# Reordering the queues of a fused attention and expert layer: fp32 products together, m behind f2, expert 0 last

## The reference

```python
q, k, v = xn @ q_w, xn @ k_w, xn @ v_w                      # 32 columns each
scores = (q @ k.T) * decay_weights                          # strictly causal, decays with distance
att = (scores @ v) @ o_w.T * out_scale
logits = xn @ router_w + router_b + load_balancer           # 4 experts, the best 2 by softmax
e0 = silu(xn @ sw_w1) * (xn @ sw_w3) @ sw_w2                # 512 hidden
e1 = gelu(sym @ me_c1w + me_c1b) @ me_c2w + me_c2b          # sym: three linear maps of xn; 256 hidden
h2 = layer_norm(syn + attn)                                 # syn, attn: linear maps of xn
h2 = layer_norm(h2 + relu(h2 @ ce_f1w + ce_f1b) @ ce_f2w + ce_f2b)
e2 = h2 @ ce_gen_w + ce_gen_b
e3 = gelu(xn @ ml_w1 + ml_b1) @ ml_w2 + ml_b2               # 512 hidden
out = x + att + sum of the two chosen experts, weighted
```

## Time and profile before

| what | us |
|---|---|
| median of 3 runs | 475.91 (475.39 to 476.07) |
| the profiled execution's own time | 475.9 |
| its span, first to last instruction | 474.1 |
| PE busy | 456.7 (96%) |
| DVE busy | 389.5 (82%) |
| ACT busy | 271.3 (57%) |
| POOL busy | 251.8 (53%) |

### The profile page before, as it was taken

The page is one execution under the profiler, slowest core; times in us unless marked ns, Lnnn a source line. Parts: engine busy times, 40 slices in busy tenths (PEclk is TensorE's granted clock), DMA queues, the critical chain, the costliest instruction groups (busy, mean ns, idle before and its releaser), DMA issues.

```text
span 474.1 us, 9536 instructions
## 1 busy us (share of the span) xinstructions
PE 456.7 (96%) x2892; PEld 381.9 (81%) x2892; DVE 389.5 (82%) x1292; ACT 271.3 (57%) x534; POOL 251.8 (53%) x370
## 2 busy tenths in 40 slices
PE   3879999999999999999999999999999999999994
PEld 2758888897888889788888878878898888878884
DVE  4567988979798897988889798888979888886994
ACT  3582846548284663829457383845728375482831
POOL 4692645737265572726657273664726357471541
PEclk9999999999999999999999999999999999999999
DMA  7300010010101001010000101001010100100000
GB/s 264 18 6 19 2 45 2 1 45 2 46 0 37 7 0 44 0 44 0 21 23 0 44 0 44 0 3 41 0 44 0 44 0 0 44 1 22 3 24 22
DMA packets 18786, 11.43 MB, mean 24 GB/s; under 512 B 1136, under 2 KB 18256, under 8 KB 18768
## 3 DMA queue, kind: packets, MB, share of 16 engines
q1 hardware_dynamic: 18480, 11.20, 8.8%
q10 hardware_dynamic: 288, 0.01, 0.0%
HBM read 6.80 MB, written 4.19 MB: 23 GB/s over the span
## 4 chain that ended last, share of the span: by engine, by line
issue 48%; POOL 36%; POOLq 11%; PE 2%; DVE 1%; ACT 1%; DMA 1%; DVEq 0%
POOL hid3l L430 14%; POOL hidl L434 9%; POOLq L398 7%; POOL n L400 5%; POOL xn L400 5%; POOLq L443 2%; POOLq L396 2%; POOL rstd_u L444 1%; DMA ROW<-rows 1%; POOL negmean_x L395 0%; POOL negmean_c L395 0%; DVE falling L604 0%; PE TR L892 0%; POOL WL L416 0%; ACT hid L523 0%
## 5 line engine op out<-in xcount | busy, mean ns | idle before, releaser
L967 PE MATMUL S<-xh,WH 128*128 128x512 f32 x224 | 98.7, 441 | 2.1 <-ACT hid L523 2.1
L969 PE MATMUL S<-xh,WL 128*128 128x512 f32 x224 | 88.5, 395 | 0.0
L968 PE MATMUL S<-xl,WH 128*128 128x512 f32 x224 | 88.1, 393 | 0.0
L430 POOL TENSOR_TENSOR hid3l<-hid,hid3h 128x512 fp32r<-128x512 f32 x64 | 80.2, 1283 | 0.0
L394 POOL TENSOR_TENSOR veps_x<-mv_x,eps 128x4 f32<-128x4 f32 x16 | 3.2, 199 | 120.9 <-DVE mv_x L582 120.9
L560 ACT ACTIVATE hid<-S,me_b 128x512 f32<-128x512 f32 x32 | 22.1, 689 | 67.4 <-PE S L969 67.3
L925 PE MATMUL EX<-scaled,hid 128*128 128x128 f32 x512 | 59.8, 275 | 0.0
L925 PEld LDWEIGHTS EX<-scaled,hid 128*128 128x128 f32 x512 | 58.4, 192 | 0.0
L967 PEld LDWEIGHTS S<-xh,WH 128*128 128x128 f32 x224 | 42.2, 188 | 18.8 <-issue 3.6
L679 DVE SCALAR_TENSOR_TENSOR OUT<-EX,coef,OUT 128x128 f32<-128x128 f32 x192 | 53.7, 341 | 0.7
L738 DVE SCALAR_TENSOR_TENSOR gate<-th,S 128x512 f32<-128x512 f32 x64 | 43.8, 685 | 8.7 <-ACT th L505 7.8
(11 more groups left out here) (171 smaller groups left out, 1079.2 us busy)
## 6 DMA issues: line engine op xcount, KB each, us to landing
X<-x SPq DMA_DIRECT2D x16, 256.0 KB, 3.0
out<-OUT SPq DMA_DIRECT2D x16, 256.0 KB, 2.4
W<-weights SPq DMA_DIRECT2D x1, 768.0 KB, 8.2
W<-weights SPq DMA_DIRECT2D x1, 512.0 KB, 5.7
W<-weights SPq DMA_DIRECT2D x1, 384.5 KB, 6.7
W<-weights SPq DMA_DIRECT2D x1, 384.0 KB, 6.2
W<-weights SPq DMA_DIRECT2D x1, 192.5 KB, 4.5
W<-weights SPq DMA_DIRECT2D x1, 162.0 KB, 4.4
```

The costliest lines, as they stand in the source:

```text
L430: pool.tensor_tensor(hid3l[:, j, :], hid[3][:, j, :], hid3h[:, j, :], ALU.subtract) \
L967: pe.matmul(bank[:, :], wh, hi, start=True, stop=False)
L968: pe.matmul(bank[:, :], wh, lo, start=False, stop=False)
L969: pe.matmul(bank[:, :], wl, hi, start=False, stop=True).then_inc(unit_ready, 1)
```

## The change

Only orders change. No operation is added or taken out, but for hidh, which is cast in two halves with a semaphore step each.

- PE: `gates(1)` comes before the transposes of n1; expert1 before st; expert2 between st and found; m0 and m1 directly behind f2; the transposes of u before expert0, which is last. In the first turn the folds of weights move behind sc and behind `gates(3)`.
- `UNITS`: a1 and b1 ahead of st.
- ACT: kd ahead of the copies of K; `half_gate(1)` ahead of h2; `half_gate(2)` ahead of hidh, `half_gate(3)` behind it and ahead of the routing's tanh; `take_x` behind the gelus of m.
- DVE: expert 0's mix ahead of qd and `masked_scores`; `u_combine` behind `silu(1)`; `silu(2)`, `silu(3)` and coef ahead of `expert2_scale` and OUT = ATT + X; `x_moments` ahead of the mix of expert 3.
- POOL: `root_u` behind hid3l.

```diff
-UNITS = ["tok0", "tok1", "tok2", "tok3", "a0", "b0", "c0", "c1", "c2", "c3", "sc", "st",
-         "a1", "b1", "f1_0", "f1_1", "a2", "b2", "a3", "b3", "e3", "f2", "m0", "m1"]
+UNITS = ["tok0", "tok1", "tok2", "tok3", "a0", "b0", "c0", "c1", "c2", "c3", "sc", "a1",
+         "b1", "st", "f1_0", "f1_1", "a2", "b2", "a3", "b3", "e3", "f2", "m0", "m1"]
...
                 norm("c", pl, n1, c_normed)
-                if not first:
-                    root_u(g.prev())
...
-                pool.wait_ge(hid_high, g.count(1, 1))
+                if not first:
+                    root_u(g.prev())
                 for j in range(2):
+                    pool.wait_ge(hid_high, g.count(2, j + 1))
                     pool.tensor_tensor(hidl[:, j, :], hid[2][:, j, :], hidh[:, j, :], ALU.subtract) \
...
                 half_gate(0)
-                act.copy(K[0:C, :], qk_bank[3 * C:4 * C, :])
-                act.copy(K[C:2 * C, :], qk_bank[3 * C:4 * C, :]).then_inc(qk_high, 1)
...
                 act.mul(kd[:, :, :], kv[:, 1:NT, 0:C], depth[:, 0:1]).then_inc(kd_ready, 1)
+                act.copy(K[0:C, :], qk_bank[3 * C:4 * C, :])
+                act.copy(K[C:2 * C, :], qk_bank[3 * C:4 * C, :]).then_inc(qk_high, 1)
...
+                half_gate(1)
                 act.wait_ge(c_turned, g.count(1, 1))
...
                 act.copy(h2h[:, :], h2[:, :]).then_inc(h2_high, 1)
-                half_gate(1)
...
-                act.wait_ge(released[g.bank("f1_1")], g.uses_before("f1_1") + 1)
-                act.copy(hidh[:, :, :], hid[2][:, :, :]).then_inc(hid_high, 1)
+                half_gate(2)
+                for j in range(2):
+                    act.wait_ge(released[g.bank(f"f1_{j}")], g.uses_before(f"f1_{j}") + 1)
+                    act.copy(hidh[:, j, :], hid[2][:, j, :]).then_inc(hid_high, 1)
+                half_gate(3)
                 act.wait_ge(lean_ready, g.count(1, 1))
                 act.activation(tlean[:, :, :], lean[:, :, :], ACT.Tanh).then_inc(tlean_ready, 1)
-                half_gate(2)
-                half_gate(3)
...
-                if not last:
-                    take_x(g.next())
                 for j in range(2):
                     m, free = unit(f"m{j}")
                     act.activation(hid[1][:, j, :], m[:, :], ACT.Gelu, bias=me_b[:, j:j + 1]).then_inc(free, 1)
+                if not last:
+                    take_x(g.next())
...
+                if not first:
+                    expert0(g.prev())
                 if first:
                     dve.wait_ge(mask_loaded, (1 + BEHIND) * DMA_INC)
...
-                if not first:
-                    expert0(g.prev())
-                if not first:
-                    u_combine(g.prev())
                 dve.wait_ge(h2_high, g.count(1, 1))
                 dve.tensor_tensor(h2l[:, :], h2[:, :], h2h[:, :], ALU.subtract).then_inc(h2_low, 1)
                 silu(1)
+                if not first:
+                    u_combine(g.prev())
...
                 if not first:
                     expert1(g.prev())
+                silu(2)
+                silu(3)
+                if first:
+                    fold_last()
+                dve.wait_ge(tlean_ready, g.count(1, 1))
+                route(dve.scalar_tensor_tensor(out=coef[g.par][:, :, :], in0=tlean[:, :, :], scalar=1.0,
+                                               in1=half[:, :, :], op0=ALU.add, op1=ALU.mult))
                 if not first:
                     expert2_scale(g.prev())
...
                     .then_inc(att_added, 1)
-                silu(2)
-                dve.wait_ge(tlean_ready, g.count(1, 1))
-                route(dve.scalar_tensor_tensor(out=coef[g.par][:, :, :], in0=tlean[:, :, :], scalar=1.0,
-                                               in1=half[:, :, :], op0=ALU.add, op1=ALU.mult))
-                silu(3)
-                if first:
-                    fold_last()
...
-                mix(g, 3, bias1_added)
                 if two_more(g):
                     x_moments(Group(g.pair, g.off + 2))
+                mix(g, 3, bias1_added)
...
-                if first:
-                    fold_first()
...
                 ins.then_inc(unit_ready, 1)
+                if first:
+                    fold_first()
+                gates(1)
                 for t in range(NT):
                     pe.wait_ge(c_normed, g.count(NT, t + 1))
                     ins = pe.transpose(TR[:, t * P:(t + 1) * P], n1[:, t, :], ident[:, :])
                 ins.then_inc(c_turned, 1)
+                if not first:
+                    expert1(g.prev())
                 pe.wait_ge(kd_ready, g.count(1, 1))
                 bank = fill("st")
...
                 ins.then_inc(unit_ready, 1)
-                gates(1)
+                if not first:
+                    expert2(g.prev())
                 if first:
                     fold_second()
-                if not first:
-                    expert1(g.prev())
...
                 ins.then_inc(found_ready, 1)
-                if not first:
-                    expert2(g.prev())
...
-                if first:
-                    fold_last()
                 gates(2)
                 gates(3)
+                if first:
+                    fold_last()
...
+                if first:
+                    pe.wait_ge(setup_took, len(TAKEN))
+                three("m0", SPLIT["me"], h, l)
+                three("m1", SPLIT["me"] + P, h, l)
                 pe.wait_ge(route_step, g.count(ROUTE_STEPS, ROUTE_STEPS - 1))
...
                 expert3(g)
+                b = g.bank("f2")
+                pe.wait_ge(released[b], g.uses_before("f2") + 1)
+                pe.wait_ge(att_added, g.count(1, 1))
+                for t in range(NT):
+                    ins = pe.transpose(ATT[:, t, :], u[:, t * P:(t + 1) * P], ident[:, :])
+                ins.then_inc(u_turned, 1)
...
                 expert0(g)
-                if first:
-                    pe.wait_ge(setup_took, len(TAKEN))
-                three("m0", SPLIT["me"], h, l)
-                three("m1", SPLIT["me"] + P, h, l)
-                b = g.bank("f2")
-                pe.wait_ge(released[b], g.uses_before("f2") + 1)
-                pe.wait_ge(att_added, g.count(1, 1))
-                for t in range(NT):
-                    ins = pe.transpose(ATT[:, t, :], u[:, t * P:(t + 1) * P], ident[:, :])
-                ins.then_inc(u_turned, 1)
```

More of the change, by code:

```diff
@@ L1039, in turn @@
                 pe.matmul(qk_bank, found[:, :], back[:, :], start=True, stop=True).then_inc(att_ready, 1)
+                gates(2)
+                gates(3)
                 if first:
                     fold_last()
-                gates(2)
-                gates(3)
                 if first:
@@ L1069, in turn @@
                 expert3(g)
-                if first:
-                    pe.wait_ge(half_done, 1)
-                    pe.wait_ge(setup_took, len(TAKEN))
-                expert0(g)
-                if first:
-                    pe.wait_ge(setup_took, len(TAKEN))
-                three("m0", SPLIT["me"], h, l)
-                three("m1", SPLIT["me"] + P, h, l)
                 b = g.bank("f2")
@@ L1083, in turn @@
                 ins.then_inc(u_turned, 1)
+                if first:
+                    pe.wait_ge(half_done, 1)
+                    pe.wait_ge(setup_took, len(TAKEN))
+                expert0(g)
             def tail(g):
```

## The result

The changed kernel takes **480.22 us** in the median of 6 runs (478.12 to 481.36), the kernel before 475.82 beside it (475.39 to 477.05): a ratio of 1.0083 (95% interval 1.0059 to 1.0108), 0.8% slower, +4.4 us. A second series of the same kernel gave 481.91 against 477.12 (1.0104, 1.0079 to 1.013). Forecast were 488.1, slower, with a range of 474.5 to 490.5. The sign holds and the range holds the time, but the likeliest case is not the one that came: the step that brings 13.6 of the forecast's +12.2 (the rest is savings) happened in one turn of fifteen of the profiled execution.

The account below looks back on a forecast made before the run. PE, busy 96% of the span, was taken to bound the kernel. PE's sequence -0.5, u +2.0, q/k +11.6 and the tail -0.9 summed to +12.2 on 475.9: 488.1 us, range 474.5 to 490.5.

Parts of the forecast that it names:

- the likeliest case: coef on DVE is held by POOL in each turn, giving 488.1 us; chance 0.55.
- The step that failed: DVE's coef comes 0 to 0.3 us behind POOL's second hidl and is held until 262.3.
- Both clocks: Summed times of POOL's second hidl taking over and of coef's request on DVE: 261.01 for each.
- Held in some turns only: Rival: the loop's two turns differ, so coef is held in half of them; 481.6 us, chance 0.13.
- The price of a hold: A held coef delays PE by 0.13 us at u in 15 turns and 0.89 at q/k after 13: 2.0 and 11.6.
- the rival: coef slips in ahead of POOL's second hidl, PE not waiting except at late landings; 475.1 us, not slower, chance 0.24.
- Except where a landing is late (some 0.6 in all): If coef is not held, only late landings of x make PE wait, some 0.6 us in all.
- PE's term: PE from the scores to the second f1 product gets 0.03 us shorter a turn, -0.5 in 15; fp32/fp32r seams are free.
- The wait for h2: DVE, done with pr, stands 1.6 us before h2l; hidden, cost 0.
- The tail: At the end m and u lie ahead of expert0, so mix 0 starts 0.2 us behind expert0: -0.9 us.
- The seams do pay: Rival: each fp32 to fp32r change on PE costs 0.08 us, two fewer a turn save 2.6: 472.4 us, chance 0.03.
- A further wait: Rival: PE meets another wait beside those counted, as at f2 or f1; above 490.5 us, chance 0.05.

Follow-up runs that it names:

- experiment 3: Changed kernel with two small DVE aggregations that nobody reads put ahead of coef, to hold it on purpose: 493.39 us, ratio 1.0366.
- experiment 7: Changed kernel with two unread DVE aggregations ahead of coef and SP issuing the load of x before the store: 477.98 us, ratio 1.004.
- experiment 10: The changed kernel repeated with nothing altered: 481.91 us, ratio 1.0104.
- experiment 8: kernel 1 with x's fp32 transposes moved between the fp32r products m0 and m1, two more type changes a turn: 476.13 us, ratio 0.9998.
- kernel 1: Changed kernel with SP issuing the load of x before the store of the turn before: 475.88 us, ratio 0.9992.
- kernel 5: Changed kernel with m0, m1, u's transposes, expert0 and ACT's take of x in the old order, x_moments behind mix 3: 476.26 us, ratio 1.0001.
- experiment 4: Kernel before with only m0 and m1 behind f2, u's transposes and expert0 last, and ACT's take of x behind m: 476.47 us, ratio 0.9992.
- experiment 9: Kernel before with m0 and m1 behind f2, u's transposes and expert0 last, x's take behind m, load of x before the store: 476.08 us, ratio 0.9994.

## Why the prediction was right and wrong

**The step that failed: "coef comes 0 to 0.3 behind the second hidl and is held until 262.3; I take that value, because each doubtful term can only delay coef."** Both clocks were right to about 0.1 us. Measured from the scores' start (248.23 in the turn of the rows, so that the forecast's 261.01 is 12.78), coef's request is at 12.81 to 12.87 and the second hidl would start at 12.82 to 12.89. Over the nine traces with this order (135 turns behind the first) I took the recorded starts: where coef's stands 7 ns or more ahead of the second hidl's, it got in each time (50 of 50) and lasted 0.17; at 6 to 1 ns ahead, in 45 of 49 (the four others: 1.33); at 3 ns behind, in one of 2; at 4 ns or more behind, it was held each time (34 of 34, of which 30 with the two aggregations in front). Where it got in just ahead, hidl's own record is up to 0.03 longer (1323 against 1297 ns): then it is POOL that stands. The one who asks first goes, and here the two ask within 0.05 us of each other. "Each doubtful term can only delay coef" was no reason: the terms of POOL's clock had rounding of their own, and the rows resolve 0.01. A sum that ends in 261.01 against 261.01 gives no chance of 0.55 to "held in each turn"; what it supports is a mix in which the shares are unknown. Of the forecast's 13.6 for the hold (11.6 + 2.0), 0.7 came in the profiled run (0.61 + 0.11) and 2.9 in the repeat (2.41 + 4 x 0.11). What made the kernel slower was mostly the landings, which the forecast had at 0.6 and in another case; that its sign came true is for the greater part luck.

**"Held in some turns only"** was the right kind of case, with 0.13 too small a chance, and its 481.6 is close to the 480.2 and 481.9 measured, but for a wrong reason: it had half of the turns held and 0.6 for the landings.

**The price of a hold: right.** +0.89 at q/k and +0.13 at u were forecast; 0.58 to 0.96 and 0.10 to 0.11 were measured (first profile, experiments 3, 7, 10). Both prices hold 0.04 to 0.05 between DVE's end and PE that the text doesn't name (265.81 against 265.72 is 0.09, not 0.13); in the first profile PE starts 0.06 behind the end of stats_u where it waited for it. The chain was right at each link: DVE waits for x in 13 turns, stats_x starts 0.02 behind the landing, mix 3 stands behind it. With coef in time the wait is there too (0.6 to 0.8 in ten of the 13 turns; the others are behind the hold and the two slow landings) and leaves 0.1 to 0.3 before PE wants q/k, as the rival had it.

**"Except where a landing is late (some 0.6 in all)": mis-sized.** It is 3.3 to 3.4, and 5.0 with the clock. I priced all loads with the median of 3.0. Two loads of the kernel before landed in 4.5 and 3.8 already, beside the same instruction packets: DVE waited 0.70 and 0.28 for them, and PE lost nothing, since x_moments stood last in DVE's turn. A median is the wrong row for a wait that will have no slack: the longest landings decide.

**PE's term: -0.03 forecast, +0.03 measured.** The seams were right: free between full tiles (experiment 8), and as many narrow drains as before. Missed was that a1 now stands behind the 96-row scores, where the transposes of n1 stood. In turn 10 of the changed kernel:

```profile
310.04 0.59 PE L1002 MATMUL S<-Q,K 96*128 96x128 f32 x4
310.47 0.45 PE L968 MATMUL S<-xh,WH 128*128 128x512 f32 x1
310.76 0.39 PE L969 MATMUL S<-xl,WH 128*128 128x512 f32 x1
```

The first product takes 0.29 instead of 0.234. From there to the second f1 product are 5.96 (310.47 to 316.43), before 5.93. The row for it was in the trace of before: the four transposes that stood in that place took 0.55 (248.66 to 249.21) and not 4 x 0.109, and I took the plain price as if the predecessor didn't matter.

**The wait for h2: right**, on DVE 1.9 instead of 1.6, and hidden (kernels 1 and 5 have it in every turn and lose nothing). **The tail: right**, -0.80 for -0.9. From the last tok (443.54), expert 0's products end at 27.65, where those of expert 1 begin, and mix 0 starts at 27.85; before 25.73 and 28.65.

```profile
471.19 1.95 PE L946 MATMUL EX<-W,hid 128*128 128x128 f32 x16
```

```profile
471.39 1.13 DVE L680 SCALAR_TENSOR_TENSOR OUT<-EX,coef,OUT 128x128 f32<-128x128 f32 x4 [1.88 <-PE EX L926]
```

**"The seams do pay": refuted** by experiment 8. **"A further wait": none came.**

## What to carry to other kernels

When an order makes a transfer's landing the last thing that a strict queue waits for, take the slack from the slowest landings in the trace and not from the median, and ask first whether the transfer can be issued sooner: one swap on SP gave back all of the 4.4 us (480.22 to 475.88). Where two engines reach for the same thing within a few hundredths of a microsecond, don't decide the race from the rows: give the outcome as a mix, price it once, and move one of the two by 0.2 us in the kernel, so that it is no race. And test the parts of a change alone before you judge them: here the first half cost nothing, the second saved 0.8 at the end, and one moved line made the first's delay count. And where executions differ in their granted clock, compare those with a like clock: the 0.8 shows there and not in the medians over all.

## What was unexpected of the hardware

- A packet of 16 KB of instructions beside a load of 256 KB brings its landing from 2.9 to 4.6 to 5.2 us (changed kernel, both series), in the same two turns each time; with the load ahead, the load took 2.9 and the store behind it 4.3. Over all twelve traces, the 15 of 168 loads issued in a turn that such a packet overlapped landed in 2.87 to 5.15, those with no instruction packet beside them in 2.57 to 3.15. In the packets of the transfer itself the last ones start only when the instruction packet has ended. No run took the packet away.
- The order of DVE and POOL at coef is decided within some 5 ns, and both can lose: DVE 1.2 to 1.3 us, or POOL 0.03. The Trainium skill, SBUF — State Buffer, SBUF: two separate sides, has it that who starts first keeps the ports for the whole instruction; the 0.17 and 1.33 agree.
- PE's clock fell to 1.2 GHz for 3.4 us behind a delay of 1.76 at q/k in turn 4 and one of 2.33 in experiment 3, but not behind one of 2.16 in turn 2 of experiment 3 nor one of 1.72 in turn 4 of the repeat. In turn 0 it fell behind a wait of 2.1 in experiments 4 and 9, and not behind the same wait in the trace of the kernel before. It costs 1.6 a time, nearly as much as the pause itself. What decides it stays open.
